# Reordering a graph layer's steps: all first layers in one run, node tiles prepared a step ahead

## The reference

```python
h = jnp.maximum(_layernorm(x, axis=-1), 0.0)
rel_inputs = concatenate([h[src], h[dst], edge_attr], axis=-1)      # 25000 x 384
rel_effects = relu(rel_inputs @ re_w1 + re_b1) @ re_w2 + re_b2      # 256 hidden, 128 out
agg = segment_sum(rel_effects, dst, num_segments=50000)
upd = relu(concatenate([h, agg], axis=-1) @ ea_w1 + ea_b1) @ ea_w2 + ea_b2
return x + upd
```

## Time and profile before

| | us |
|---|---|
| median of 3 runs | 987.33 (987.01 to 987.4) |
| the profiled execution | 985.56 |
| its span in the profile | 983.8 |
| TensorE busy | 932.3 (95%) |
| VectorE busy | 737.0 (75%) |
| ScalarE busy | 549.7 (56%) |
| GpSimd busy | 582.1 (59%) |

### The profile page before, as it was taken

One profiled execution on the slowest core, in us unless ns is written; L12 is line 12 of the kernel. 1 busy time (PEld: TensorE's weight loads), 2 busy tenths in 40 slices (PEclk: granted clock), 3 DMA queues, 4 the chain that ended last, 5 costly groups with the idle time before them and its releaser, 6 DMA issues.

```text
span 983.8 us, 19952 instructions
## 1 busy us (share of the span) xinstructions
PE 932.3 (95%) x5994; PEld 827.9 (84%) x5994; DVE 737.0 (75%) x2051; ACT 549.7 (56%) x1083; POOL 582.1 (59%) x609
## 2 busy tenths in 40 slices
PE   1577999999999999999999999999999999999997
PEld 1456888889889888988988988888988988898876
DVE  3665878778777778878877887877887777887652
ACT  1134566556566556656656656656656655665653
POOL 6883566566567566566566656656656656655121
PEclk9978999999999999999999999999999999999999
DMA  4324454454454454454444445445445445434331
GB/s 135 98 78 121 136 160 128 135 164 135 128 165 141 123 166 143 122 163 138 134 148 151 136 140 157 131 139 161 132 130 165 140 125 166 142 121 151 92 108 55
DMA packets 114340, 132.90 MB, mean 135 GB/s; under 512 B 18084, under 2 KB 70250, under 8 KB 114224
## 3 DMA queue, kind: packets, MB, share of 16 engines
q1 hardware_dynamic: 101440, 105.43, 34.7%
q0 software_dynamic: 12784, 26.10, 9.3%
HBM read 92.46 MB, written 39.00 MB: 134 GB/s over the span
## 4 chain that ended last, share of the span: by engine, by line
PE 91%; POOL 4%; DVE 2%; issue 1%; ACT 1%; SPq 0%; DMA 0%; POOLq 0%; DVEq 0%
PE l_ps L502 32%; PE l_ps L520 26%; PE l_ps L510 16%; PE agg_ps L474 9%; PE edge_ps L458 4%; PE node_ps L466 4%; POOL gath L364 2%; POOL picked_i L406 0%; DVE st L715 0%; POOL lo L385 0%; DMA dst_all<-in_dst_cols 0%; DMA win<-rel_rows 0%; ACT hid L623 0%; DVE res L787 0%; SPq L270 0%
## 5 line engine op out<-in xcount | busy, mean ns | idle before, releaser
L380 POOL TENSOR_TENSOR xb<-xin,b2n 128x512 f32<-128x512 f32 x98 | 126.7, 1293 | 256.9 <-DVE res L787 256.9
L364 POOL DMA_INDIRECT gath<-in_x,src_all x196 | 191.8, 979 | 55.8 <-issue 50.2
L364 POOL DMA_INDIRECT gath<-in_x,dst_all x196 | 186.0, 949 | 61.4 <-issue 61.4
L623 ACT ACTIVATE hid<-l_ps,b1e 128x512 f32<-128x512 f32 x98 | 67.3, 687 | 226.6 <-PE l_ps L510 226.6
L623 ACT ACTIVATE hid<-l_ps,b1n 128x512 f32<-128x512 f32 x196 | 134.6, 688 | 103.8 <-PE l_ps L510 103.7
L520 PE MATMUL l_ps<-w2n,hid 128*128 128x128 f32 x1568 | 191.0, 275 | 0.8 <-ACT hid L623 0.8
L520 PEld LDWEIGHTS l_ps<-w2n,hid 128*128 128x128 f32 x1568 | 186.5, 192 | 5.7 <-ACT hid L623 1.2
L753 DVE TENSOR_SCALAR h<-gath,rs,shift 128x128 f32<-128x128 f32 x392 | 177.2, 520 | 1.8
L502 PE MATMUL l_ps<-hi,w1n_hi 128*128 128x512 f32 x392 | 167.2, 427 | 1.5 <-ACT hid L623 1.5
L630 ACT ACTIVATE h<-xin,shift,rs 128x128 f32<-128x128 f32 x392 | 160.3, 482 | 0.1
L502 PE MATMUL l_ps<-hi,w1n_lo 128*128 128x512 f32 x392 | 154.8, 395 | 0.0
(11 more groups left out here) (78 smaller groups left out, 1293.1 us busy)
## 6 DMA issues: line engine op xcount, KB each, us to landing
win<-rel_rows SPq DMA_DIRECT2D x392, 66.0 KB
xin<-in_x_tiles SPq DMA_DIRECT2D x98, 256.0 KB, 4.4
out<-res SPq DMA_DIRECT2D x98, 256.0 KB, 2.0
rel_rows<-rel_row SPq DMA_DIRECT2D x49, 264.0 KB, 2.2
ea_in<-in_ea_t SPq DMA_DIRECT2D x49, 256.0 KB, 4.3
gath<-in_x,src_all POOLq DMA_INDIRECT x196, 2.5
gath<-in_x,dst_all POOLq DMA_INDIRECT x196, 2.6
w1e<-in_L_gnn_re_w SPq DMA_DIRECT2D x1, 384.0 KB, 3.5
```

The costliest lines, as they stand in the source:

```text
L364: nc.gpsimd.indirect_dma_start(gath[b][:, s, k, :], None, x, bass.IndirectOffsetOnAxis(ap=idx[:, e * T + k:e * T + k + 1], axis=0)).then_i ...
L380: nc.gpsimd.tensor_tensor(xb[r][:, :, :], xin[r][j % 2][:, :, :], b2[1][:, :].unsqueeze(1).to_broadcast([P, T, D]), ALU.add).then_inc(xb_s ...
L623: nc.scalar.activation(hid[r][:, c, :], l1_ps[c][:, :], ACT.Relu, bias=b[:, c:c + 1]).then_inc(hid_set, 1)
```

## The change

TensorE's joint step now does all six first-layer halves in a row, and then all float32 work: transposes and sum of the next pair's tile 1, edge transposes, edge layer 2, tile 1 layer 2, transposes and sum of the next pair's tile 2, tile 2 layer 2. Both tiles' features and sums are so made a step ahead, and `enter` makes both for pair 0. The pair step is laid out alike. The edge attributes' high and low parts get two buffers each (`ea_hi`, `ea_lo`), and the high part for e + 1 is made at the start of step e on ScalarE. The other engines' lists are reordered to go with it: VectorE does all statistics first, then tile 2's last result, then all edge normalisations and both marks; ScalarE spreads tile 1's normalisations between the hiddens; GpSimd puts `low_ea` and tile 2's `keep_x` behind the first four of eight gathers; SyncE loads both windows first. The diff, cut to its core:

```diff
-        parts = [3, 2, 2]
-        order = [(2, 0, 1), (0, 1), (0, 1)]
+        parts = [2, 2, 2]
...
+        ea_hi = [sb(f"ea_hi{b}", [P, G], F32R) for b in range(2)]
+        ea_lo = [sb(f"ea_lo{b}", [P, G], F32R) for b in range(2)]
...
             def joint_step(e, j):
-                if j + 1 < NJ:
-                    load_window(1, j + 1)
+                for r in (1, 2):
+                    if j + 1 < NJ:
+                        load_window(r, j + 1)
+                if e + 2 < EG:
+                    load_ea(e + 2)
                 if j > 0:
                     store(2, j - 1, True)
-                if e + 2 < EG:
-                    load_ea(e + 2)
                 for r in (1, 2):
                     if j + 2 < NJ:
                         load_x(r, j + 2)
-                if j + 1 < NJ:
-                    load_window(2, j + 1)
                 store_rel(e, True)
                 store(1, j, True)
...
             def low_ea(e):
                 pool.wait_ge(ea_hi_set, e + 1)
-                nc.gpsimd.tensor_tensor(lo[0][:, 2, :], ea_in[e % 2][:, :], hi[0][:, 2, :].bitcast(F32), ALU.subtract).then_inc(ea_lo_set, 1)
+                nc.gpsimd.tensor_tensor(ea_lo[e % 2][:, :], ea_in[e % 2][:, :], ea_hi[e % 2][:, :].bitcast(F32),
+                                        ALU.subtract).then_inc(ea_lo_set, 1)
...
             def joint_step(e, j):
                 set_dst(e)
+                if e + 2 < EG:
+                    gather(e + 2, range(0, 2))
+                if e + 1 < EG:
+                    low_ea(e + 1)
                 if j > 0:
                     keep_x(2, j, True)
                 if e + 2 < EG:
-                    gather(e + 2)
-                if e + 1 < EG:
-                    low_ea(e + 1)
+                    gather(e + 2, range(2, T))
                 if j + 1 < NJ:
                     keep_x(1, j + 1, True)

...
+                if r == 0:
+                    srcs = [(2, ea_hi[n % 2][:, :], ea_lo[n % 2][:, :], (ea_hi_set, n + 1), (ea_lo_set, n + 1)),
...
             def enter(fast):
-                if fast:
-                    pe.wait_ge(split[1], 1)
-                    pe.wait_ge(loaded[1], LOADS)
-                    turn_nodes(1, 0)
-                    sum_window(1, 0)
-                else:
-                    pe.wait_ge(split[1], 1)
-                    pe.wait_ge(loaded[1], LOADS)
-                    turn_nodes(1, 0)
-                    sum_windows(1, 0)
+                pe.wait_ge(split[1], 1)
+                pe.wait_ge(loaded[1], LOADS)
+                for r in (1, 2):
+                    turn_nodes(r, 0)
+                    (sum_window if fast else sum_windows)(r, 0)
+

             def joint_step(e, j):
                 turn = edge_turn(e, True)
-                layer1(0, e, turn, 0)
-                layer1(0, e, turn, 1)
-                turn_nodes(2, j)
-                sum_window(2, j)
-                layer1(1, j, turn + 1, 0)
-                layer1(1, j, turn + 1, 1)
-                layer2(0, turn)
-                layer1(2, j, turn + 2, 0)
-                layer2(1, turn + 1)
-                if e + 1 < EG:
-                    turn_edges(e + 1)
-                layer1(2, j, turn + 2, 1)
+                for r, n in ((0, e), (1, j), (2, j)):
+                    for c in range(C):
+                        layer1(r, n, turn + r, c)
                 if j + 1 < NJ:
                     turn_nodes(1, j + 1)
                     sum_window(1, j + 1)
+                if e + 1 < EG:
+                    turn_edges(e + 1)
+                layer2(0, turn)
+                layer2(1, turn + 1)
+                if j + 1 < NJ:
+                    turn_nodes(2, j + 1)
+                    sum_window(2, j + 1)
                 layer2(2, turn + 2)

             def pair_step(j, fast):
                 turn = node_turn(1, j, fast)
                 add = sum_window if fast else sum_windows
-                turn_nodes(2, j)
-                add(2, j)
-                layer1(1, j, turn, 0)
-                layer1(1, j, turn, 1)
-                layer1(2, j, turn + 1, 0)
-                layer2(1, turn)
-                layer1(2, j, turn + 1, 1)
+                for r in (1, 2):
+                    for c in range(C):
+                        layer1(r, j, turn + r - 1, c)
                 if j + 1 < NJ:
                     turn_nodes(1, j + 1)
                     add(1, j + 1)
+                layer2(1, turn)
+                if j + 1 < NJ:
+                    turn_nodes(2, j + 1)
+                    add(2, j + 1)
                 layer2(2, turn + 1)

...
                 act.wait_ge(ea_loaded[e % 2], 16 * (e // 2 + 1))
-                if e > 0:
-                    act.wait_ge(l1_done, C * edge_turn(e - 1, fast) + C)
-                nc.scalar.activation(hi[0][:, 2, :], ea_in[e % 2][:, :], ACT.Copy).then_inc(ea_hi_set, 1)
+                if e > 1:
+                    act.wait_ge(l1_done, C * edge_turn(e - 2, fast) + C)
+                nc.scalar.activation(ea_hi[e % 2][:, :], ea_in[e % 2][:, :], ACT.Copy).then_inc(ea_hi_set, 1)
...
             def enter(fast):
                 act.wait_ge(loaded[1], LOADS)
-                high_nodes(1, 0, fast)
+                for r in (1, 2):
+                    high_nodes(r, 0, fast)

             def joint_step(e, j):
                 turn = edge_turn(e, True)
+                more = j + 1 < NJ
+                if e + 1 < EG:
+                    high_ea(e + 1, True)
                 hidden(0, turn, 0, before_edge(e, True))
+                if more:
+                    deviations(e + 1, slice(0 if e + 1 < EG else 2 * T, ST))
                 hidden(0, turn, 1, before_edge(e, True))
-                high_nodes(2, j, True)
-                if e + 1 < EG:
-                    high_ea(e + 1, True)
+                if more:
+                    normalise(1, j + 1, True, range(0, 1))
                 hidden(1, turn + 1, 0, before_node(1, j, True))
-                if j + 1 < NJ:
-                    deviations(e + 1, slice(0 if e + 1 < EG else 2 * T, ST))
+                if more:
+                    normalise(1, j + 1, True, range(1, 3))
                 hidden(1, turn + 1, 1, before_node(1, j, True))
-                if j + 1 < NJ:
-                    normalise(1, j + 1, True)
+                if more:
+                    normalise(1, j + 1, True, range(3, T))
                 hidden(2, turn + 2, 0, before_node(2, j, True))
-                if j + 1 < NJ:
+                hidden(2, turn + 2, 1, before_node(2, j, True))
+                if more:
+                    high_nodes(1, j + 1, True)
+                if e + 1 < EG:
+                    high_edges(e + 1)
+                if more:
                     normalise(2, j + 1, True)
-                if e + 1 < EG:
-                    high_edges(e + 1)
-                hidden(2, turn + 2, 1, before_node(2, j, True))
-                if j + 1 < NJ:
-                    high_nodes(1, j + 1, True)
+                    high_nodes(2, j + 1, True)

             def pair_step(j, fast):
                 turn = node_turn(1, j, fast)
-                if j + 1 < NJ:
+                more = j + 1 < NJ
+                if more:
                     deviations(stats_turn(j + 1, fast), slice(2 * T, ST))
-                high_nodes(2, j, fast)
                 hidden(1, turn, 0, before_node(1, j, fast))
                 hidden(1, turn, 1, before_node(1, j, fast))
-                if j + 1 < NJ:
+                if more:
                     normalise(1, j + 1, fast)
                 hidden(2, turn + 1, 0, before_node(2, j, fast))
                 hidden(2, turn + 1, 1, before_node(2, j, fast))
-                if j + 1 < NJ:
+                if more:
+                    high_nodes(1, j + 1, fast)
                     normalise(2, j + 1, fast)
-                    high_nodes(1, j + 1, fast)
+                    high_nodes(2, j + 1, fast)
...
+            def low_nodes(r, j):
+                low_features(r, j)
+                low_sums(r, j)
+
             def enter(fast):
-                if fast:
-                    mark(1, 0)
-                    mark(2, 0)
-                else:
-                    mark_all(1, 0)
-                low_features(1, 0)
-                low_sums(1, 0)
+                for r in (1, 2):
+                    (mark if fast else mark_all)(r, 0)
+                    low_nodes(r, 0)

             def joint_step(e, j):
+                more = j + 1 < NJ
                 what = (e + 1, some(e + 1, EG), some(j + 1, NJ))
+                statistics(*what)
+                totals(*what)
+                squares(*what)
+                spreads(*what)
                 if j > 0:
                     node_results(2, j - 1, True)
-                statistics(*what)
-                totals(*what)
-                low_features(2, j)
-                squares(*what)
-                low_sums(2, j)
-                spreads(*what)
-                mark(1, j + 1)
```

(87 more changed lines are left out.)

25 lines of the change are left out of this document (12 added, 13 removed).

## The result

The changed kernel takes **1034.91 us** (median of 4 runs, 1034.63 to 1035.92) where the kernel before, run beside it on the same chip, takes 987.17 (4 runs, 985.52 to 987.4): a ratio of 1.0489, interval 1.0471 to 1.0507. The profiled execution was 1034.66 us with a span of 1032.8; before's span was 983.8, so 49.0 us have to be found. The forecast was 987.2, its range 984 to 1029. The change is slower, by the first rival's mechanism, and by more than that rival's price.

The account below looks back on a forecast made before the run. PE work was taken to bound the joint steps, unchanged at 18.65 of 18.68 us. Switches -0.5, entry +3.3 and pair steps -2.9 gave -0.1: 987.2 us on the median's scale, range 984 to 1029.

Parts of the forecast that it names:

- the first rival: Joint steps: shift waits for POOL's second addition too, PE stands 0.85 us in each of 45 steps; +38, 1025 us; chance 0.25.
- the PE's sum: Joint step: matmuls, second layers, transposes and window sums add to 18.65 of 18.68 us, all moved and none removed.
- The three breaks saved: Joint steps: three fewer entries into float32r per step, 0 to 0.01 us each, 0 to -1.4 us over 46 steps; taken -0.5.
- Shift is let in between.: Joint step: DVE's shift runs between POOL's two adjacent additions, ends at t = 5.5, and the step stays at 18.67 us.
- the row that I called thin: Before's profile: DVE's addition at 57.84 ended at 58.50 while POOL's following copy ran 58.41 to 58.61; evidence for letting in.
- A smaller collision: Joint steps, slower rival: addition over the spread, up to 0.9 us a step, or slack overdrawn; 992 to 1005 us; chance 0.13.
- The entry: Start of the joint part: PE must wait for tile 2's window mark before its sum; +3.3 us, bounds 2 to 4.
- The pair steps: Three steps at the end: 4.8 us idle removed, 1.9 of new waits; -2.9 us, bounds -1.5 and -4; two steps of 12.7.
- The two waits that I named: Pair steps: PE waits for tile 2's normalised blocks (0.44 us) and tile 2's mark (0.45 us), in two steps.
- no idle: Pair steps: hidden(1,0) runs 2.06 to 2.75, PE wants it at 2.8, so PE does not wait there.

## Why the prediction was wrong

**What bounds the kernel, and the PE's sum: right.** The step of 18.68 came back in every kernel without the collision (18.68 and 18.70 in turn with all gathers first or one addition moved, 18.68 to 18.74 with the shift first). The three breaks saved bring nothing. I had taken -0.5 for them; the joint parts without collision were 840.1 to 841.5 against 839.73, so +0.4 to +1.8. 0.4 to 0.6 of it is that every second step or so is 18.70 or a little more; where it was 1.6 and 1.8 (one addition moved, gathers between), the two steps with POOL's gap add 0.6 to 0.7 each.

**The step that failed: "Shift is let in between."** All times around it were right to 0.1 us (t = 0 is 520.16): the shift was asked at t = 4.21 (4.2 forecast), POOL's additions began at 4.06 and 5.31 (4.15 and 5.4), the rival's shift ended at 6.63 (6.7), hidden(1,0) at 7.75 (7.8). What failed was the choice between two ends by the row that I called thin, the copy at 58.41. That copy is 128 x 4 and came after a DVE operation on one element; the runs show that DVE is not let in between two adjacent POOL additions, whether it is the shift or the mark that waits. The rows for the rival were the better ones, the fourth normalisation held ahead of the addition's record, and the runs show the same with the square, the mark and, in the two steps with POOL's gap, the shift itself (asked at 306.17, the first addition's record from 306.76). The Trainium skill (SBUF — State Buffer, "Who interferes with whom") says that whoever issues first gets the shared port pair for the whole instruction. That one holds the other off agrees with every run here. The order of issue, as far as the rows show it, does not: the shift, asked at 524.37, would have gone ahead of an addition begun at 525.47, and it did not. Were the second addition also to take hold some 0.67 before its record, at about 524.8, the first would still be running, and POOL would never let go between them; but the shift was asked before that too. What decides it inside the chip was not shown.

**The rival's price was too low** (1025 against 1034.9). It had the wait, 0.85 (0.82 in 41 steps), and lacked the restart: 1.21 instead of 0.93 for the first four matmuls. 43 steps x (0.86 + 0.27) = 48.6, 0.86 being the mean with the two longer waits, and the stage shows 48.5; 45 x 0.85 was 38.

**The chance.** 0.25 for a rival whose mechanism had two rows for it, against 0.47 resting on one thin row, was the wrong way round. The range, 1029, was closed at the rival's price with 4 us on top, while its price left out what a stopped PE pays on restart. The chain of before had that number, in the pair steps: the four matmuls behind a wait for hidden took 1.19, and 0.94 in a row without a wait.

```profile
945.22 1.19 PE l_ps L502 x4
```

**A smaller collision** did not happen in the changed kernel, but it is what the run with the break shows: 0.6 earlier in the step (t = 3.5, not 4.06), and the addition lands on the square.

**The entry.** I took +3.3, bounds 2 to 4, on the scale with 1.33 more work done. After: 104.18 - 100.59 - 1.33 = +2.3. The window's mark came at 82.67 and not 83.45, and the clock had risen. In the other kernels with this entry and the same first joint step it was +2.6 (three additions) and +3.2 to +4.5, above my bound in two (+4.4 and +4.5: one addition moved, gathers between), both with the clock at its lower level over the sum and the six matmuls behind it (2.05 and 2.56; 1.13 and 1.40 in the changed kernel). The late statistics of the first step cost the PE 0.57 (0.5 forecast) and a restart. The mechanism (the PE waits for tile 2's mark) is as forecast:

```profile
83.51 1.13 PE L476 MATMUL agg_ps<-hot,win 128*128 128x128 f32 x8 [1.52 <-DVE hot L798]
```

**The pair steps** gave less: -3.05 with 1.33 less work in them, so -1.7 by the scale on which I forecast -2.9 (bounds -1.5 and -4). Steps were 13.36 and 13.35, not 12.7. Timeline of the changed kernel:

```profile
1001.90 0.63 PE L468 MATMUL node_ps<-ident,h 128*128 128x128 f32 x4 [0.53 <-ACT h L627]
...
1002.85 0.91 PE L476 MATMUL agg_ps<-hot,win 128*128 128x128 f32 x6 [0.32 <-DVE hot L798]
```

The two waits that I named are there with 0.53 and 0.32 (0.44 and 0.45 forecast); the term was mis-sized because each restart adds its 0.2 to 0.27 (the transposes take 0.63 and not 0.44, the sum 1.13 and not 0.89), and because a third one stands at 995.2, where I had written "no idle": hidden is ready just as the PE comes to it, and four matmuls take 1.19 though the PE hardly stands: the weight load before them waited 0.42 for hidden.

## What to carry to other kernels

Where an engine is already full and its operations take the same time in any order, as the PE's did in the joint steps, reordering it can't gain; it can only lose, because every move shifts short operations of other engines against each other. What there was to gain lay at the ends, in the pair steps. So before such a move, list for every short DVE operation on the way to the bottleneck which POOL operations with SBUF operands run beside it, and keep two of those from standing next to each other there: a pair of gathers or a wait between them took the loss away (1034.9 to 991.1 and less). Leave room for a POOL list that comes 0.8 later now and then. Price a new wait of the PE as its idle time plus the restart (0.27 us here for 512-column matmuls, 0.2 for transposes), and where one thin row decides between no loss and 5%, give the loss the larger chance or let the range hold all of it.

## What was not expected of the hardware

- Adjacent POOL additions hold a waiting DVE operation with two SBUF inputs to the end of the last: with one, two and three of them it took 1.17, 2.42 and 3.42 us, an operation of 0.17. A gather behind an addition does not extend the hold (1.17), and eight normalisations beside gathers alone took 2.14 in the changed kernel.
- Behind a gather, an addition's hold begins about 0.67 us before its record does: a mark asked 0.66 before it was held, one asked 0.68 before it was not.
- In all kernels here POOL stood 1.06 to 1.15 us instead of 0.30 between two gathers at the same two of the 46 joint steps; the cause is not known.
- After a stop of 0.4 to 1.8 us the PE needs about 0.27 us more for the first 512-column matmul (0.50 from start to end, where an unbroken run gives 0.233 each), 0.24 more for a sum (0.32 us stop) and 0.19 for four transposes (0.53 and 1.00). It costs that (1.19 against 0.93 for four) even where the PE stands no measurable time but its weight load had to wait.
- Going between float32 and float32r costs nothing that these runs can show: one change per step or four, 18.68 and 18.70 in turn against 18.68.
- The granted clock at the entry differed between kernels with the same entry (0.89 in the changed kernel, 0.53 with one addition moved away, both from 80 to 90 us); e = 4 began at 104.18 and 106.31.
